# Adding the causal mask in VectorE's row-maximum instruction instead of with a TensorE matmul

## The reference, cut to what matters

```python
# x: (8, 512, 512); LN = layernorm without gain
x = x + 0.5 * ffn(LN(x))          # ffn: gate and up 512 -> 2048, silu(gate) * up, down 2048 -> 512
x = x + attention(LN(x))
x = x + 0.5 * ffn(LN(x))
# attention, per batch, 16 heads of 32 columns:
qkv = x @ w_qkv;  q, k = rope(unit_norm(q)), rope(unit_norm(k))   # rope on every second head
logits = einsum(q, k) * q_gain                                    # (16, 512, 512)
logits = where(column <= row, logits, finfo.min)                  # the causal mask
y = softmax(logits) @ v;  return y @ w_out
```

## Time and profile before

| | |
|---|---|
| median of 3 runs | 2815.13 us (2815.12 to 2816.86) |
| the profiled execution | 2815.85 us, its span 2814.0 us |
| PE | 98% busy, 23232 matmuls |
| DVE | 62% busy, 4158 instructions |
| ACT, POOL | 43%, 19% |
| granted PE clock | 0.995 of full speed over the span |
| DMA | 39.37 MB, 14 GB/s in the mean |

### The profile page before, as it was taken

The page is one execution under the profiler, slowest core; times in us unless marked ns, Lnnn a source line. Parts: engine busy times, 40 slices in busy tenths (PEclk is TensorE's granted clock), DMA queues, the critical chain, the costliest instruction groups (busy, mean ns, idle before and its releaser), DMA issues.

```text
span 2814.0 us, 56217 instructions
## 1 busy us (share of the span) xinstructions
PE 2749.1 (98%) x23232; PEld 2024.6 (72%) x23232; DVE 1756.3 (62%) x4158; ACT 1208.5 (43%) x2250; POOL 530.7 (19%) x820
## 2 busy tenths in 40 slices
PE   4999999999999999999999999999999999999999
PEld 4677777777777777777767777677777777777776
DVE  7766666666656566566656666566666757676643
ACT  5443444354434444343434445334443445354422
POOL 0012132213130302203121121211203131313100
PEclk8999999999999999999999999999999999999999
DMA  6000000000000000000000000000000000000000
GB/s 256 1 16 1 16 1 1 1 16 16 1 1 16 16 1 1 1 16 16 2 1 9 9 16 1 1 16 8 9 1 16 16 2 1 1 16 6 4 9 16
DMA packets 16574, 39.37 MB, mean 14 GB/s; under 512 B 1472, under 2 KB 1472, under 8 KB 15808
## 3 DMA queue, kind: packets, MB, share of 16 engines
q1 hardware_dynamic: 16320, 35.79, 3.6%
HBM read 26.35 MB, written 9.44 MB: 13 GB/s over the span
## 4 chain that ended last, share of the span: by engine, by line
PE 89%; DVE 8%; ACT 2%; issue 1%; DMA 0%; POOL 0%; SPq 0%; DVEq 0%; ACTq 0%
PE psum L1042 26%; PE psum L1044 26%; PE psum L1043 26%; PE psum L1173 2%; PE psum L1196 2%; PE psum L1208 2%; PE psum L1065 1%; PE psum L1155 1%; PE psum L1151 1%; PE psum L1174 1%; DVE mneg L936 1%; DVE arena L886 1%; DVE arena L884 1%; PE psum L1209 1%; DVE arena L957 1%
## 5 line engine op out<-in xcount | busy, mean ns | idle before, releaser
L1042 PE MATMUL psum<-arena,WG 128*128 128x256 f16 x2048 | 558.7, 273 | 4.9 <-DVE arena L886 3.5
L1044 PE MATMUL psum<-arena,WG 128*128 128x256 f16 x2048 | 558.7, 273 | 0.0
L1043 PE MATMUL psum<-arena,WG 128*128 128x256 f16 x2048 | 558.6, 273 | 0.0
L1042 PE MATMUL psum<-arena,WU 128*128 128x256 f16 x2048 | 558.4, 273 | 0.0
L1044 PE MATMUL psum<-arena,WU 128*128 128x256 f16 x2048 | 558.4, 273 | 0.0
L1043 PE MATMUL psum<-arena,WU 128*128 128x256 f16 x2048 | 558.3, 273 | 0.0
L884 DVE SCALAR_TENSOR_TENSOR arena<-arena,psum 128x256 f32<-128x256 f32 x512 | 214.9, 420 | 481.2 <-ACT arena L776 480.3
L776 ACT ACTIVATE arena<-psum,tscale 128x256 f32<-128x256 f32 x512 | 242.6, 474 | 588.0 <-PE psum L1044 587.4
L1042 PE MATMUL psum<-WD,arena 128*128 128x512 f16 x1024 | 388.2, 379 | 3.9 <-DVE arena L890 3.9
L1044 PE MATMUL psum<-WD,arena 128*128 128x512 f16 x1024 | 388.0, 379 | 0.0
L1043 PE MATMUL psum<-WD,arena 128*128 128x512 f16 x1024 | 387.9, 379 | 0.0
(11 more groups left out here) (147 smaller groups left out, 4531.3 us busy)
## 6 DMA issues: line engine op xcount, KB each, us to landing
arena<-in_L_attn_x SPq DMA_DIRECT2D x16, 512.0 KB, 3.7
out<-arena SPq DMA_DIRECT2D x16, 512.0 KB, 2.8
arena<-in_L_ffn_w_gate SPq DMA_DIRECT2D x4, 1024.0 KB, 9.4
arena<-in_L_ffn_w_up SPq DMA_DIRECT2D x4, 1024.0 KB, 6.5
WD<-in_L_ffn_w_down SPq DMA_DIRECT2D x4, 1024.0 KB, 10.7
arena<-in_L_attn_w_qkv SPq DMA_DIRECT2D x1, 3072.0 KB, 21.5
arena<-in_L_attn_w_out SPq DMA_DIRECT2D x1, 1024.0 KB, 5.4
park<-arena SPq DMA_DIRECT2D x2, 512.0 KB, 2.8
```

Of the source, the lines that this page charges most:

```text
L1042: T_.matmul(o, lhs(0), rhs(0), start=first, stop=False)
L1043: T_.matmul(o, lhs(0), rhs(1), start=False, stop=False)
L1044: return T_.matmul(o, lhs(1), rhs(0), start=False, stop=last)
```

## The change

The mask becomes 512 columns wide: `maskq` is 0 in columns 0 to 383 and has the triangle in the last 128. `scores_max` issues no mask matmul any more. `row_max` replaces each TENSOR_REDUCE by a `tensor_tensor_reduce`: it reads the scores in PSUM and the last w columns of `maskq` in SBUF, adds them, writes the sum back to the same place in PSUM and the row maximum to `mneg`. Ahead of each bank's instructions stands a `memset` of one column of a new tile `carrier`, the first instruction behind the wait for PE. The maxima are no longer negated, so `maxima` multiplies by -2^-12. Four helper tiles of the prologue now share the columns of `ss`, `ss2`, `rn` and `mneg`, and `gain` shrinks. MANY["end values"] goes from 1 to 0.5, FEW["end"] from 1 to 0.8.

```diff
-    maskq = sb("maskq", P, BF16)
+    maskq = sb("maskq", S, BF16)
-    gain = sb("gain", 5 * H, F32)
+    gain = sb("gain", 2 * H, F32)
-    wmax = sb("wmax", 32, F32)
-    wpow = sb("wpow", 32, F32)
-    wrec = sb("wrec", 32, F32)
-    wscale = sb("wscale", 32, F32)
+    carrier = sb("carrier", 3, F32)
+    wmax, wpow, wrec, wscale = ss, ss2, rn, mneg
+    FUSED = range(B)
...
-            "head": 1, "end": 1, "end values": 1, "out 0": 1, "out 1": 2, "out 2": 1, "out 3": 1}
+            "head": 1, "end": 1, "end values": 0.5, "out 0": 1, "out 1": 2, "out 2": 1, "out 3": 1}
...
-           "head": 0.56, "end": 1, "end values": 1, "out 0": 1.25, "out 1": 1.25, "out 2": 1, "out 3": 1.5}
+           "head": 0.56, "end": 0.8, "end values": 1, "out 0": 1.25, "out 1": 1.25, "out 2": 1, "out 3": 1.5}
...
-            nc.gpsimd.affine_select(out=maskq[:, :], in_=maskq[:, :], compare_op=ALU.is_ge, fill=MASKED,
+            nc.gpsimd.affine_select(out=maskq[:, S - P:S], in_=maskq[:, S - P:S], compare_op=ALU.is_ge, fill=MASKED,
...
             def row_max(b, hf, h, bank):
                 dve.wait_ge(s["s1_ps"], 3 * head_no(b, hf, h) + bank + 1)
+                if b in FUSED:
+                    V_.memset(carrier[:, bank:bank + 1], 0.0)
                 for t in QBANKS[bank]:
-                    ins = V_.tensor_reduce(mnegv[:, t, h:h + 1], ps(0, QSEG[t], (t + 1) * P), AX_X, ALU.max, negate=True)
+                    w, col = (t + 1) * P, mnegv[:, t, h:h + 1]
+                    ins = V_.tensor_tensor_reduce(out=ps(0, QSEG[t], w), in0=ps(0, QSEG[t], w), in1=maskq[:, S - w:S], scale=1.0, scalar=2 * MASKED,
+                                                  op0=ALU.add, op1=ALU.max, accum_out=col) if b in FUSED else V_.tensor_reduce(col, ps(0, QSEG[t], w), AX_X, ALU.max, negate=True)
                 ins.then_inc(s["smax_done"], 1)
...
-                src = mnegv[:, :, g * GH:(g + 1) * GH]
+                src, unit = mnegv[:, :, g * GH:(g + 1) * GH], -2.0 ** -12 if b in FUSED else 2.0 ** -12
...
-                        T_.matmul(ps(0, QSEG[t], w), QT[0:ST, h, t * P:(t + 1) * P], KT[0:ST, h, 0:w], start=True, stop=False)
-                        ins = T_.matmul(ps(0, QSEG[t] + t * P, P), identb[:, :], maskq[:, :], start=False, stop=True)
+                        ins = T_.matmul(ps(0, QSEG[t], w), QT[0:ST, h, t * P:(t + 1) * P], KT[0:ST, h, 0:w], start=True, stop=b in FUSED)
```

More of the change, by code:

```diff
@@ L813, in _ @@
             dve.wait_ge(s["c_in"], 32)
-            g0, g1, g2, g3, g4 = (gain[:, i * H:(i + 1) * H] for i in range(5))
+            g0, g4, g1, g2, g3 = gain[:, 0:H], gain[:, H:2 * H], ss[:, 0:H], ss2[:, 0:H], rn[:, 0:H]
             link(V_.tensor_scalar(g1.bitcast(I32), g0.bitcast(I32), 0x7FFFFFFF, None, ALU.bitwise_and))
@@ L915, in unit @@
                 dve.wait_ge(s["qs_done"], i + 1)
-                chained(V_.tensor_tensor(rn[:, 16 * b2:16 * b2 + HH], rn[:, 16 * b2:16 * b2 + HH], gain[:, 4 * H + hf * HH:4 * H + (hf + 1) * HH], ALU.mult))
+                chained(V_.tensor_tensor(rn[:, 16 * b2:16 * b2 + HH], rn[:, 16 * b2:16 * b2 + HH], gain[:, H + hf * HH:H + (hf + 1) * HH], ALU.mult))
                 V_.tensor_tensor(qn[b2].rearrange("p (h c) -> p h c", c=HD), qs[b2].rearrange("p (h c) -> p h c", c=HD),
@@ L944, in maxima @@
                     dve.wait_ge(s["mt_ps"], k)
-                src = mnegv[:, :, g * GH:(g + 1) * GH]
-                chained(V_.tensor_scalar(mstv[:, :, :, 0], src, 2.0 ** -12, None, ALU.mult))
-                V_.scalar_tensor_tensor(out=mstv[:, :, :, 1], in0=src, scalar=2.0 ** -12, in1=mstv[:, :, :, 0], op0=ALU.mult, op1=ALU.subtract).then_inc(s["mst_done"], 1)
+                src, unit = mnegv[:, :, g * GH:(g + 1) * GH], -2.0 ** -12 if b in FUSED else 2.0 ** -12
+                chained(V_.tensor_scalar(mstv[:, :, :, 0], src, unit, None, ALU.mult))
+                V_.scalar_tensor_tensor(out=mstv[:, :, :, 1], in0=src, scalar=unit, in1=mstv[:, :, :, 0], op0=ALU.mult, op1=ALU.subtract).then_inc(s["mst_done"], 1)
             def max_rows(b, hf, g):
@@ L1172, in scores_max @@
                         w = (t + 1) * P
-                        T_.matmul(ps(0, QSEG[t], w), QT[0:ST, h, t * P:(t + 1) * P], KT[0:ST, h, 0:w], start=True, stop=False)
-                        ins = T_.matmul(ps(0, QSEG[t] + t * P, P), identb[:, :], maskq[:, :], start=False, stop=True)
+                        ins = T_.matmul(ps(0, QSEG[t], w), QT[0:ST, h, t * P:(t + 1) * P], KT[0:ST, h, 0:w], start=True, stop=b in FUSED)
+                        if b not in FUSED:
+                            ins = T_.matmul(ps(0, QSEG[t] + t * P, P), identb[:, :], maskq[:, S - P:S], start=False, stop=True)
                     ins.then_inc(s["s1_ps"], 1)
```

## The result

The changed kernel takes 2797.29 us (2796.95 to 2798.85), the kernel before 2815.13: a ratio of 0.9937, interval 0.9925 to 0.9949, so 17.8 us less, where 9.7 less were forecast. The profiled execution took 2798.85 us, the longest of the four; its span is 2797.1 us at a granted clock of 0.994.

The account below looks back on a forecast made before the run. PE's instruction stream was taken as the bound, busy 98% of the span. 28.2 - 12.1 - 5.2 - 1.2 = 9.7 us off 2815.1 gave 2805.4 us, range 2793 to 2832.

Parts of the forecast that it names:

- Mask matmuls: In PE's stream: 512 mask matmuls leave at 0.055 us each, a gain of 28.2 us if PE never waits more.
- rival D: In PE's stream: weight loads come out from under the masks, so their place is not given back; no separate chance.
- d: DVE's added time per head from the new row maxima: 0.28 us, with ends 0 and 0.90.
- (a): DVE's main row-maximum instruction: second source and full-width output cost nothing against the reduce, at 512 columns or below.
- (b) and (c): On DVE per head: taking out four maxima and three carrier memsets, seven additions at 0.04 us each.
- First stretches: 16 stretches of four heads' row maxima, in four kinds named by example start time: 12.1 us lost to waits for DVE.
- Second groups: Heads 4 to 7, 16 groups: PE waits after the last head's maxima, 5.2 us lost.
- Other waits: PE's other waits for DVE, at the splits, come later at a few places: 1.2 us lost, an estimate.
- The shares: Fill settings, 0.5 and 0.8 instead of 1: no fill point moves more than about a quarter piece, 0 in the mean.
- Slope and break-even: First stretches and last heads pass on 60 us per us of d; the gain is used up at d = 0.44.
- Rival A: DVE has room: the additions vanish in the overlap, d about 0.10, 20.5 us gained, 2795 us; chance 0.13.
- Rival C: DVE bounds first stretches: each maximum's readout waits for an empty pipeline, d = 0.78, 2835 us; chance 0.22.

Follow-up runs that it names:

- E4: The kernel before without mask matmuls and with its plain reduce, row maxima taken over masked columns too: 2792.14 us.
- E6: The changed kernel with one more DVE reduce over 192 mask columns per head, read by nobody: 2809.22 us.
- E1: The changed kernel with the two shares put back to those of the kernel before: 2800.54 us.
- E2: The kernel before with only the two new shares: 2812.64 us.
- E9: The changed kernel without memsets, and with mask matmul and plain reduce again in nine of the 16 first stretches: 2795.63 us.
- E7: The changed kernel with FEW max first at 0.45 instead of 0.32, more pieces under the short batches' first maxima: 2800.43 us.

## Why the prediction was right or wrong

The side, the mechanism and the place were right, and the time lies in the range; the size was 8.1 us off. By its own steps:

- **Mask matmuls, 28.2 us.** Undersized: 0.055 us came from one place; E4 shows 0.060, 30.7 us. +2.5. Loads came out from under nothing: rival D has no support in any run.
- **d = 0.28 us per head.** Too large: 0.17 from start to start, 0.17 to 0.19 by E6's slope. The part (a), "Second source and full-width output cost nothing", holds at 512 columns (0.01) and fails below (0.05), which I had read off a wide instruction only. The parts (b) and (c), seven times 0.04, were too dear: a memset costs about 0.01 us, and so does the whole new form at 512 columns, readout included. Some of the 0.05 at the shorter widths may be the readout's. Part (a) was too cheap and (b) and (c) too dear; that d came out within 0.11 of the forecast is in part luck.
- **First stretches, 12.1 us lost.** By stages 16 x 0.96 - 4.61 = 10.75. Kind by kind, taken against 0.96: like 1164 lost 0.21 (I had 0.35), like 2179 1.13 (1.2), like 831 1.11 (1.0), like 2309 0.82, and 1.19 in batch 0 (1.0). E4 adds what I could not see: like 2179 and 831 give only 0.29 and 0.25 even with DVE's work unchanged, with PE's stops for the maxima up from 15 to 44 in the whole kernel; more than half of that loss is not d's.
- **Second groups, 5.2 us lost.** 16 x 0.96 - 10.18 = 5.18; in E1, without the shares, 4.7. Right.
- **Other waits, 1.2 us.** The stages between the second groups and the next first stretch changed by 0.03 us in E1. No such loss is there.
- **Together** the waits take 16.1 us (7.7 for PE's early arrival, E4; 8.4 for DVE, E1 against E4; 15.4 in E1 by stages) instead of 18.5. +2.4.
- **The shares, 0.** The step that failed most: 3.25 us by E1, 2.4 by E2, 2.8 by the stages of either. That a fill point moves by no more than "about a quarter of a piece" may be so, but in batches 3 to 5 one piece jumped behind the start of a chain that ends in DVE's L908, for which PE stopped eight times in the kernel before, and that took three of these stops away. "PE dense everywhere" was read from windows of 240 and 300 us; the table of waits had the row for L908.
- **Slope and break-even.** 45 us per us of d (E6), not 60, so by this slope the gain with the old shares would be used up at about d = 0.19 + 14.6/45 = 0.51, an estimate that no run tries. At E6's d of about 0.44, where the prediction had the break-even, the kernel is still 5.9 us faster than before, or 2.7 when the shares' 3.25 are taken off.

The sum by runs: 30.7 - 7.7 - 8.4 + 3.25 = 17.8 us. It closes by construction, as each term but the first is a difference of two runs; what is measured apart is the 0.96 us per stretch behind the 30.7 and the slope of E6.

Rival A had the time nearest (2795), and its mechanism, additions that vanish, holds for the memsets and for the readout at 512 columns. That it came nearest in time is partly luck: without the shares, which A put at nothing too, the gain is 14.6 us (E1), 4.9 from the forecast and 5.9 from A.

Rival C named the right instruction: a readout of its own of 141 ns stands 512 times in the trace. Its price is another matter: the readout starts at 258.36 where the row before it ends at 258.44, and the next large instruction at 258.37, before the readout ends at 258.50. Of the two sections of the Trainium skill that the prediction took C's rules from (VectorE: DVE Perf Modes, The DRAIN you can't avoid, and Two Vector instructions with no wait between them), the rule that an output of the accumulator makes two instructions is borne out by these rows. The rule that the next one starts only when the pipeline is empty is not, and the prediction left out a condition: the first section goes on to say that an instruction that is not held starts earlier, and by the second section an instruction is held, in the main, when one of its operands starts in another group of 32 partitions than the operand last used before it in the same memory. The operands of the row maxima cover 128 partitions, so all start in the first group, and from one row maximum to the next nothing is held. So read, page and trace agree.

What stays open: why the new form costs 0.05 us at 128 to 384 columns and 0.01 at 512. No run varied the second source, the writing of the result into PSUM and the readout one apart from the others.

## What to carry to other kernels

Work moved off a bound engine returns its time only in stages where the engine behind it has room: here 0.75 of 0.96 us in the seven roomy stretches, nothing in the sum of the nine tight ones; count stage by stage, and consider keeping the old form in the tight ones (E9). Run the moved work's removal without its replacement (E4) first: it separates what can't come back from what the replacement costs. An instruction's row is not its price: at 512 columns a row of 141 ns cost 0.01 us or less from start to start. And small retimings of filler work (2.8 to 3.3 us here) need a look at the table of waits, not a mean.

## What the runs showed of the hardware that was not expected

The readout of the accumulator is hidden almost wholly at 512 columns, as told. The other point is the clock. Windows of PE in the kernel after (length, busy us and count, granted clock, DMA share, GB/s):

```profile
148.00:151.00 3.00, 1.02 (x5) 1.00 0.79 302
151.00:154.00 3.00, 2.59 (x7) 0.54 0.00 0
154.00:158.00 4.00, 4.00 (x33) 0.92 0.00 0
```

The same window of the kernel before:

```profile
151.00:154.00 3.00, 2.87 (x21) 1.00 0.00 0
```

In both kernels PE has just stood idle for 2.39 us, waiting for DVE; these are the rows behind that stop, first of the kernel after, then of the kernel before:

```profile
151.41 0.61 PE L1045 MATMUL psum<-WD,arena 128*128 128x512 f16 x1 [2.39 <-DVE arena L889]
```

```profile
151.13 0.39 PE L1042 MATMUL psum<-WD,arena 128*128 128x512 f16 x1 [2.39 <-DVE arena L890]
```

In the kernel after 0.54 was granted behind the stop, about the lower of the two levels (1.2 of 2.4 GHz), and PE issued 7 matmuls in these 3 us instead of 21. In this profiled execution that makes the prologue 1.6 us longer. The same stop of 2.39 us stands at the same matmul in all twelve profiled executions. The clock fell behind it in two of them, the changed kernel's and E7's (0.53), and stayed at 1.00 in the ten others. So the stop alone doesn't tell the two kinds apart, and what does is open. It is a reason to compare stages, not spans, where less than 2 us matter.
